# Another order of the calls in front of the loop, on all five engines

## The chip, the cores and the metric

The kernel runs on one core of a Trainium2 chip. The time is the device time of one launch in microseconds (us), the median of several runs. The core has five engines with an instruction queue each: TensorE (PE, matrix products), VectorE (DVE), ScalarE (ACT), GpSimd (POOL) and SyncE (SP), which here only starts transfers. Each queue runs in order; between queues an instruction waits on semaphores.

## The reference

The input t is 16 sequences of 1024 rows of 256 numbers. For each sequence:

```
x = x + layernorm(attention(layernorm(x)))
x = x + layernorm(ffn(layernorm(x)))

attention(t): qkv = t @ W_qkv.T + b_qkv;  Q, K, V = three parts of 256
              softmax(Q @ K.T / 16) @ V
ffn(x):       wg, wu, wd = integer weights / 127     (768 x 256, 768 x 256, 256 x 768)
              (silu(x @ wg.T) * (x @ wu.T)) @ wd.T
```

The norms have no weights and an epsilon of 1e-5.

## The kernel before

The kernel never forms Q and K. It forms A = Wq.T Wk once, z = A x per sequence (`project_z`), and the scores as z times x (`score`). Every factor of a product is split into a high and a low half of 16 bits, and the product is three matmuls: high by high, high by low and low by high. This is why each value is handled several times: ScalarE makes the float value or its high half (`x_hat`, `x_high`, `z_high`, `exp`, `p_high`, `o_high`, `y_hat`, `y_high`, `silu`, `h_high`), and GpSimd or VectorE subtracts to get the low half (`x_low`, `z_low`, `p_low`, `o_low`, `y_low`, `h_low`). SyncE then transposes both halves with a DMA (`turn_x`, `turn_p`, `turn_y`).

The second argument of each call is the sequence b. `x_stats`, `x_norm` and `x_hat` normalise its rows, in two halves g of 512 rows. `score(b, i)` gives the scores of 128 rows against all 1024, i from 0 to 7, in two PSUM banks (the fourth argument is the first bank). `row_max` (VectorE, L708 and L712) finds each row's maximum, `exp` (ScalarE, L491) the exponentials into one of two buffers P, `p_high` (L498) and `p_low` (L374) its halves in one of three buffers. `attend(b, g, u)` is a quarter of P times x for the 512 rows of half g, `project_v` the product with Wv; `y_scale`, `y_stats`, `y_norm`, `x1_add`, `x1_norm` are the first residual sum and its norms. `gate_up(b, g, c)` is one of six chunks of the hidden layer, `h_mul` multiplies gate and up, `down(b, g, pair)` is the last product and `d_stats`, `d_norm`, `d_add`, `add_bias` the second residual sum.

The FFN weights come as integers. Their largest values are found by `ffn_max`, brought into one row by `turn_max` on TensorE, rounded to powers of two by `powers` on VectorE (L616, L619, L621, L624), spread over all partitions by `spread_powers` on TensorE, and turned into scales by `ffn_scales`; `ffn_high` and `ffn_low` make the halves, `turn_ffn` transposes them. `bound` and `V_scales` do the like for the attention's weights.

The order of the work is written out by hand, as a list of calls for each engine: a part in front of the loop, then `for b in range(1, 13)` (ScalarE's from 2 to 13) with one list for all rounds, then a part behind it. A call waits for what it needs by a semaphore count: `exp` of number m waits for `row_max` of m, for `p_low` of m - 2, whose buffer P it takes; `p_high` waits for the transposes of m - 3; `score(b, i, bank, free0, free1)` waits for the two counts that say its banks are free. In the part in front of the loop the engines do sequence 0's attention, then sequence 1's scores woven with sequence 0's attention and its FFN. The lists in the code call helpers, so a line number names a helper's instruction, not its place in the order.

GpSimd takes `x_norm`, all `x_hat_pool`, most `p_low` and `h_low` (VectorE has p_low for i = 1 and 4, `PL_ON_VECTOR`), `z_low` (that of sequence 0 is on VectorE), `x_low`, `y_low` and the norms.

Of the kernel before, what the change touches and what calls it, by code (L numbers as in the profile page):

```python
# [41 lines left out]
def sandwich(nc, x_d, wqkv_d, b_d, wg_d, wu_d, wd_d, out_d):  # L42
# [8 lines left out]
    with ctx:  # L51
# [93 lines left out]
        ffn_scaled, sc2_ready, flag_ready = sem("ffn_scaled"), sem("sc2_ready"), sem("flag_ready")  # L145
# [894 lines left out]
        def _(engine):  # L1040
# [57 lines left out]
            turn_y(s, 0, 0, 1)
            turn_x(s, 2, 1, 0)
            turn_x(s, 2, 1, 1)  # L1100
            load_x(s, 3, 0)
            load_x(s, 3, 1)
            turn_p(s, 1, 5, 0)
            turn_p(s, 1, 5, 1)
            turn_p(s, 1, 6, 0)
            turn_p(s, 1, 6, 1)
            turn_y(s, 0, 1, 0)
            turn_y(s, 0, 1, 1)
            turn_p(s, 1, 7, 0)
            turn_p(s, 1, 7, 1)  # L1110
# [107 lines left out]
        def _(engine):  # L1218
# [5 lines left out]
            x_norm(p, 1, 0)  # L1224
            x_norm(p, 1, 1)
            p_low(p, 0, 0)
            x_hat_pool(p, 1, 1)
            x_low(p, 1, 0)
            p_low(p, 0, 2)
            p_low(p, 0, 3)  # L1230
# [7 lines left out]
            x_norm(p, 2, 1)  # L1238
            z_low(p, 1, 1)
            x_hat_pool(p, 2, 1)  # L1240
            y_norm(p, 0, 0)
            p_low(p, 1, 2)
            p_low(p, 1, 3)
            x1_norm(p, 0, 0)
            x_low(p, 2, 0)
            y_norm(p, 0, 1)
            y_low(p, 0, 0)
            p_low(p, 1, 5)
            x_low(p, 2, 1)
# [9 lines left out]
            z_low(p, 2, 1)  # L1259
            x_norm(p, 3, 0)  # L1260
            h_low(p, 0, 1, 0)
            h_low(p, 0, 1, 1)
            h_low(p, 0, 1, 3)
            x_norm(p, 3, 1)
            h_low(p, 0, 1, 4)
            d_norm(p, 0, 0, 0)
            d_norm(p, 0, 0, 1)
            p_low(p, 2, 0)
# [104 lines left out]
        def _(engine):  # L1373
# [10 lines left out]
            exp(a, 0, 1, 6)  # L1384
            p_high(a, 0, 1)
            x_hat(a, 1, 0)
            x_high(a, 1, 0)
            exp(a, 0, 2, 0)
            p_high(a, 0, 2)
            exp(a, 0, 3, 2)  # L1390
            x_high(a, 1, 1)
            p_high(a, 0, 3)
            exp(a, 0, 4, 4)
            p_high(a, 0, 4)
            exp(a, 0, 5, 6)
            z_high(a, 1, 0, 2)
            p_high(a, 0, 5)
            exp(a, 0, 6, 0)
            p_high(a, 0, 6)
            ffn_high(a, 0)  # L1400
            exp(a, 0, 7, 4)
            p_high(a, 0, 7)
            ffn_high(a, 1)
            exp(a, 1, 0, 0)
            o_high(a, 0, 0, 0)
            p_high(a, 1, 0)
            o_high(a, 0, 0, 1)
# [49 lines left out]
            h_high(a, 0, 1, 3)
            silu(a, 0, 1, 5, 0)
            h_high(a, 0, 1, 4)
            x_hat(a, 3, 0)  # L1460
            h_high(a, 0, 1, 5)
            x_hat(a, 3, 1)
            exp(a, 2, 0, 0)
            p_high(a, 2, 0)
            o_high(a, 1, 0, 1)
            add_bias(a, 0, 0, 0)
            o_high(a, 1, 0, 0)
            add_bias(a, 0, 0, 1)
# [211 lines left out]
        def _(engine):  # L1680
# [9 lines left out]
            x_low(v, 0, 1)  # L1690
            A_low(v)
            c_scales(v)
            V_row_sizes(v)
            bound(v, 1)
            V_scales(v)
            z_float(v, 0, 0, 0)
            z_low(v, 0, 0)
            V_low(v)
            x_stats(v, 1, 0)
            row_max(v, 0, 0, 4)  # L1700
            x_stats(v, 1, 1)
            row_max(v, 0, 1, 6)
# [510 lines left out]
```

## Time and profile before

| | |
|---|---|
| median of 3 runs | 1368.16 us (1368.06 to 1368.95) |
| the profiled execution | 1369.69 us |
| its span, first to last instruction | 1367.9 us |
| mean granted clock of TensorE | 0.997 |
| busy: PE, DVE, ACT, POOL | 1350.2, 901.9, 875.9, 826.5 us |
| DMA, share of 16 engines' span (main queue) | 55.3% |

The profile is of one execution. "Busy" is the time in which an engine works on an instruction; an instruction that waits for a semaphore is not counted, one that has begun and is held up is. A row of the timeline may merge neighbours of one kind (x4) and gives the idle time before it with what ended it. "Releasers" are inferred; where the row says "issue", the profile shows none. PEclk is the granted clock of TensorE as a share of 2.4 GHz.

### The profile page before, as it was taken

What the parts mean: (1) busy time and instruction counts of PE and PEld (TensorE: products, weight loads), DVE (VectorE), ACT (ScalarE), POOL (GpSimd) and SP (SyncE); (2) the same over time, 40 slices, a digit from 0 to 9 for tenths busy, and PEclk for the clock granted to TensorE, in tenths of its full rate; (3) what the DMA queues carried; (4) which work ended last, traced back from release to release, by engine and by line L of the source; (5) the groups of instructions that cost most, each with busy time, mean ns of one, the idle gap of its engine ahead of it and who ended that gap; (6) DMA issues with size and microseconds to landing.
All of it is one profiled execution on the core that took longest, in us unless ns stands there. A gap on an engine that the chain in (4) does not pass through costs nothing.

```text
span 1367.9 us, 22383 instructions
## 1 busy us (share of the span) xinstructions
PE 1350.2 (99%) x7406; PEld 726.3 (53%) x7406; DVE 901.9 (66%) x2169; ACT 875.9 (64%) x1374; POOL 826.5 (60%) x1003
## 2 busy tenths in 40 slices
PE   8999999999999999999999999999999999999998
PEld 4444455554555555555554555545555555555555
DVE  7876565766756667666766666667576676656556
ACT  5667575656756667575675756667566675746645
POOL 4677384674837658476484755748376584754635
PEclk9999999999999999999999999999999999999999
DMA  8995382745728456382764736547373563725512
GB/s 212 198 183 131 72 161 78 128 119 94 146 78 146 94 118 137 78 164 67 133 138 70 162 78 121 126 87 145 85 138 102 112 137 85 136 65 101 108 32 63
DMA packets 437192, 158.29 MB, mean 116 GB/s; under 512 B 418129, under 2 KB 420561, under 8 KB 437074
## 3 DMA queue, kind: packets, MB, share of 16 engines
q1 hardware_dynamic: 436272, 156.03, 55.3%
q8 instruction: 61, 1.00, 0.3%
q10 hardware_dynamic: 802, 0.79, 0.2%
q14 instruction: 57, 0.47, 0.1%
HBM read 36.70 MB, written 16.78 MB: 39 GB/s over the span
## 4 chain that ended last, share of the span: by engine, by line
PE 89%; DVE 4%; SPq 3%; DMA 2%; issue 1%; ACT 1%; POOL 0%; DVEq 0%; ACTq 0%; POOLq 0%
PE S L837 88%; SPq L268 1%; DMA yTl<-yl 1%; DVE mxs L708 1%; SPq L249 1%; DVE S L737 1%; DVE st L746 0%; DVE st L690 0%; SPq L274 0%; DMA xs<-in_L_attn_t 0%; ACT Ph L498 0%; DMA xTl<-xl 0%; SPq L237 0%; DVE zw L701 0%; POOL yl L401 0%
## 5 line engine op out<-in xcount | busy, mean ns | idle before, releaser
L491 ACT ACTIVATE P<-S,nmx,sc 128x1024 f32<-128x1024 f32 x128 | 153.6, 1200 | 285.4 <-DVE nmx L712 285.4
L708 DVE TENSOR_REDUCE mxs<-S 128x1 f32<-128x1024 f32 x128 | 156.0, 1218 | 120.5 <-PE S L837 120.5
L774 DVE SCALAR_TENSOR_TENSOR hf<-S,sc,hf 128x512 f32<-128x512 f32 x192 | 141.8, 745 | 138.7 <-ACT hf L526 133.3
L374 POOL TENSOR_TENSOR Pl<-P,Ph 128x1024 f16<-128x1024 f32 x96 | 204.4, 2130 | 36.0 <-issue 26.3
L837 PE MATMUL S<-xTh,zTh 128*128 128x512 f16 x512 | 194.7, 380 | 4.7 <-ACT P L491 2.2
L837 PE MATMUL S<-xTl,zTh 128*128 128x512 f16 x512 | 194.8, 380 | 0.0
L837 PE MATMUL S<-xTh,zTl 128*128 128x512 f16 x512 | 194.2, 380 | 0.0
L837 PE MATMUL S<-PTh,xh 128*128 128x512 f16 x512 | 194.1, 379 | 0.0
L837 PE MATMUL S<-PTl,xh 128*128 128x512 f16 x512 | 194.0, 379 | 0.0
L837 PE MATMUL S<-PTh,xl 128*128 128x512 f16 x512 | 194.0, 379 | 0.0
L319 POOL TENSOR_SCALAR rs<-mv,sc 128x2 f32<-128x2 f32 (+2 forms) x96 | 35.2, 367 | 231.2 <-DVE mv L750 191.9
L837 PE MATMUL S<-Wh,hTl 128*128 128x256 f16 x768 | 170.3, 273 | 0.0
L837 PE MATMUL S<-Wh,hTh 128*128 128x256 f16 x768 | 170.3, 272 | 0.0
L410 POOL TENSOR_TENSOR hTl<-hf,hTh 128x512 f16<-128x512 f32 x128 | 146.2, 1156 | 39.2 <-ACT hTh L533 39.0
L526 ACT ACTIVATE hf<-S,sc 128x512 f32<-128x512 f32 x192 | 130.6, 681 | 51.9 <-POOL hTl L410 36.1
L323 POOL TENSOR_TENSOR rs<-rs,mhalf 128x4 f32<-128x4 f32 (+2 forms) x160 | 145.3, 908 | 13.4
L837 PE MATMUL S<-yTh,Gh 128*128 128x512 f16 x384 | 145.6, 379 | 3.1 <-DMA yTl<-yl 1.7
L837 PE MATMUL S<-yTl,Gh 128*128 128x512 f16 x384 | 145.5, 379 | 0.0
L837 PE MATMUL S<-yTh,Uh 128*128 128x512 f16 x384 | 145.5, 379 | 0.0
L837 PE MATMUL S<-yTl,Uh 128*128 128x512 f16 x384 | 145.5, 379 | 0.0
L533 ACT ACTIVATE hTh<-hf 128x512 f16<-128x512 f32 x192 | 119.8, 624 | 34.8 <-DVE hf L774 34.8
L498 ACT ACTIVATE Ph<-P 128x1024 f16<-128x1024 f32 x128 | 135.1, 1055 | 3.5
(145 smaller groups left out, 2473.0 us busy)
## 6 DMA issues: line engine op xcount, KB each, us to landing
xs<-in_L_attn_t SPq DMA_DIRECT2D x32, 512.0 KB, 5.5
X<-in_L_attn_t SPq DMA_DIRECT2D x32, 512.0 KB, 4.5
out_x<-X SPq DMA_DIRECT2D x62, 256.0 KB, 2.9
PTh<-Ph SPq DMA_TRANSPOSE x128, 3.3
PTl<-Pl SPq DMA_TRANSPOSE x128, 3.3
hTl<-in_L_ffn_w_gate SPq DMA_DIRECT2D x1, 768.0 KB, 7.8
hTh<-in_L_ffn_w_up SPq DMA_DIRECT2D x1, 768.0 KB, 9.5
hTl<-in_L_ffn_w_down SPq DMA_DIRECT2D x1, 768.0 KB, 10.8
```

Of the source, the lines that this page charges most:

```text
L249: s.engine.dma_start_transpose(dst[k][:, gs, :, :].rearrange("p t d n -> p (t d) n"), src[k][:, gs, :].rearrange("p t d -> p (t d)")).then ...
L319: p.engine.tensor_scalar(rs, var, scalar1=eps, scalar2=mul, op0=ALU.add, **({} if mul is None else {"op1": ALU.mult})).then_inc(g_step, 1)
L323: return p.engine.tensor_tensor(out=rs, in0=rs, in1=mhalf[:, 0:rs.shape[1]], op=ALU.pow)
L374: p.engine.tensor_tensor(out=Pl[:, m % 3, :], in0=P[:, m % 2, :], in1=Ph[:, m % 3, :], op=ALU.subtract).then_inc(pl_vector if i in PL_ON_V ...
L410: p.engine.tensor_tensor(out=hTl[g][:, c, :], in0=hf[:, n % 3, :], in1=hTh[g][:, c, :], op=ALU.subtract).then_inc(hl_vector if c in HL_ON_ ...
L491: a.engine.activation(P[:, m % 2, :], ps[:, bank:bank + 2, :].rearrange("p a n -> p (a n)"), ACT.Exp, bias=nmx[:, c:c + 1], scale=sS, accu ...
L498: a.engine.activation(Ph[:, m % 3, :], P[:, m % 2, :], ACT.Copy).then_inc(ph_done, 1)
L526: a.engine.activation(hf[:, n % 3, :], ps[:, bank, :], ACT.Silu, scale=sc2[:, 3:4]).then_inc(silu_done, 1)
L533: a.engine.activation(hTh[g][:, c, :], hf[:, n % 3, :], ACT.Copy).then_inc(hh_done, 1)
L708: v.engine.tensor_reduce(mxs[:, c:c + 1], ps[:, bank:bank + 2, :].rearrange("p a n -> p (a n)"), axis=AX.X, op=ALU.max, negate=True).then_ ...
L774: v.engine.scalar_tensor_tensor(out=hf[:, n % 3, :], in0=ps[:, bank + 1, :], scalar=sc2[:, 4:5], in1=hf[:, n % 3, :], op0=ALU.mult, op1=AL ...
L837: done = t.engine.matmul(out, s, m, start=(start and i == 0), stop=(stop and i == len(terms) - 1))
```

## The change

Only the order of calls is changed, in the parts in front of the loop of all five lists; calls, helpers, the loop and the part behind it are the same. What a `score` or `gate_up` waits for is changed nowhere. On VectorE, for example, in diff form:

```
+            z_float(v, 0, 0, 0)
+            z_low(v, 0, 0)
             bound(v, 1)
             V_scales(v)
-            z_float(v, 0, 0, 0)
-            z_low(v, 0, 0)
             V_low(v)
+            row_max(v, 0, 0, 4)
             x_stats(v, 1, 0)
-            row_max(v, 0, 0, 4)
-            x_stats(v, 1, 1)
             row_max(v, 0, 1, 6)
             z_float(v, 0, 1, 2)
             row_max(v, 0, 2, 0)
+            x_stats(v, 1, 1)
+            z_low(v, 0, 1)
             p_low(v, 0, 1)
-            z_low(v, 0, 1)
             row_max(v, 0, 3, 2)
...
-            p_low(v, 0, 4)
             z_float(v, 1, 0, 2)
             powers(v, 2, 5, OB[1], 1.0, 1)
+            p_low(v, 0, 4)
+            row_max(v, 0, 7, 4)
             ffn_scales(v)
...
             y_stats(v, 0, 1, 0)
+            row_max(v, 1, 5, 2)
             y_stats(v, 0, 1, 1)
             p_low(v, 1, 4)
-            row_max(v, 1, 5, 2)
-            x1_add(v, 0, 1, 0)
             row_max(v, 1, 6, 0)
             row_max(v, 1, 7, 2)
+            x1_add(v, 0, 1, 0)
             x1_add(v, 0, 1, 1)
             h_mul(v, 0, 0, 0, 6)
-            row_inverse(v, 1, 1)
             z_float(v, 2, 0, 0)
+            x_stats(v, 3, 0)
             h_mul(v, 0, 0, 1, 2)
```

TensorE's list:

```
             score(t, 0, 6, 0, (exp_done, 3), (exp_done, 3))
+            score(t, 0, 7, 4, (exp_done, 5), (exp_done, 5))
             project_z(t, 1, 0, 2, (exp_done, 4), (exp_done, 4))
-            score(t, 0, 7, 4, (exp_done, 5), (exp_done, 5))
             turn_max(t, 2, 5, OB[1], 3, (exp_done, 6))
             attend(t, 0, 0, 0, (exp_done, 6))
             spread_powers(t, 2, 5, OB[1], 1)
             attend(t, 0, 0, 1)
+            attend(t, 0, 0, 2, (ffn_scaled, 6))
             score(t, 1, 0, 0, (exp_done, 7), (exp_done, 7))
-            attend(t, 0, 0, 2, (ffn_scaled, 6))
             attend(t, 0, 0, 3)
+            score(t, 1, 1, 2, None, None)
             project_z(t, 1, 1, 0, (exp_done, 9), (exp_done, 9))
-            score(t, 1, 1, 2, None, None)
...
+            project_z(t, 2, 0, 0, (exp_done, 15), (exp_done, 15))
             gate_up(t, 0, 0, 0, 6, (ol_done[0], 2), (ol_done[1], 2), three)
-            project_z(t, 2, 0, 0, (exp_done, 15), (exp_done, 15))
...
             gate_up(t, 0, 1, 2, 0, (silu_done, 6), (hmul_done, 6), three)
+            down(t, 0, 0, 1, (x1_done, 8), three)
+            down(t, 0, 0, 0, (x1_done, 6), three)
             gate_up(t, 0, 1, 3, 2, (silu_done, 7), (hmul_done, 7), three)
             gate_up(t, 0, 1, 4, 6, (silu_done, 8), (hmul_done, 8), three)
             gate_up(t, 0, 1, 5, 0, (silu_done, 9), (hmul_done, 9), three)
-            down(t, 0, 0, 0, (x1_done, 6), three)
-            down(t, 0, 0, 1, (x1_done, 8), three)
```

On GpSimd `x_hat_pool(1,1)` moves behind `p_low(0,2)`, `x_low(1,0)` and `p_low(0,3)`; `p_low(1,6)`, `p_low(1,7)`, `z_low(2,1)` and `x_norm(3,1)` move to its end, near `p_low(2,0)`. On ScalarE `p_high(0,6)` moves behind both `ffn_high` and `exp(0,7)`, `p_high(1,7)` behind `h_high(0,0,5)`; `exp(0,2)` moves ahead of `p_high(0,1)` and `x_hat(1,0)`. On SyncE `turn_p(1,1,0)` moves ahead of the transposes of the second and third FFN weight, and `turn_p(1,6,1)` and both `turn_p(1,7)` to the end.

VectorE at the start of the program, from `row_max(0,1)` to `z_low(0,1)`: mxs and nmx are a row_max, zw is `z_float`, zTl `z_low`, Pl `p_low`, st and mv `x_stats`. Before:

```order
L708 TENSOR_REDUCE mxs<-S 128x1
L712 TENSOR_SCALAR nmx<-mxs,sc 128x1
L701 TENSOR_SCALAR zw<-S,cb 128x512 x2
L708 TENSOR_REDUCE mxs<-S 128x1
L712 TENSOR_SCALAR nmx<-mxs,sc 128x1
L374 TENSOR_TENSOR Pl<-P,Ph 128x1024
L364 TENSOR_TENSOR zTl<-zw,zTh 128x512 x2
```

and now, the same stretch:

```order
L708 TENSOR_REDUCE mxs<-S 128x1
L712 TENSOR_SCALAR nmx<-mxs,sc 128x1
L701 TENSOR_SCALAR zw<-S,cb 128x512 x2
L708 TENSOR_REDUCE mxs<-S 128x1
L712 TENSOR_SCALAR nmx<-mxs,sc 128x1
L690 BN_STATS st<-xs 128x6 x4
L694 BN_AGGR mv<-st 128x2 x4
L364 TENSOR_TENSOR zTl<-zw,zTh 128x512 x2
L374 TENSOR_TENSOR Pl<-P,Ph 128x1024
```

The second x_stats stood ahead of these rows before and now stands between `row_max(0,2)` and `z_low(0,1)`; p_low has moved behind z_low.

VectorE from `y_scale(0,1)` on (S<-S,rinv,bvb), with `y_stats` (st<-S, mv), `p_low(1,4)` and the row_max of scores (1,5) and after. Before:

```order
L737 SCALAR_TENSOR_TENSOR S<-S,rinv,bvb 128x256 x4
L746 BN_STATS st<-S 128x6 x2
L750 BN_AGGR mv<-st 128x2 x2
L746 BN_STATS st<-S 128x6 x2
L750 BN_AGGR mv<-st 128x2 x2
L374 TENSOR_TENSOR Pl<-P,Ph 128x1024
L708 TENSOR_REDUCE mxs<-S 128x1
L712 TENSOR_SCALAR nmx<-mxs,sc 128x1
L759 SCALAR_TENSOR_TENSOR X<-S,rs,X 128x256 x2
L764 BN_STATS st<-X 128x6 x2
```

and now:

```order
L737 SCALAR_TENSOR_TENSOR S<-S,rinv,bvb 128x256 x4
L746 BN_STATS st<-S 128x6 x2
L750 BN_AGGR mv<-st 128x2 x2
L708 TENSOR_REDUCE mxs<-S 128x1
L712 TENSOR_SCALAR nmx<-mxs,sc 128x1
L746 BN_STATS st<-S 128x6 x2
L750 BN_AGGR mv<-st 128x2 x2
L374 TENSOR_TENSOR Pl<-P,Ph 128x1024
L708 TENSOR_REDUCE mxs<-S 128x1
L712 TENSOR_SCALAR nmx<-mxs,sc 128x1
L708 TENSOR_REDUCE mxs<-S 128x1
L712 TENSOR_SCALAR nmx<-mxs,sc 128x1
```

The first row_max has moved ahead of the second `y_stats` and of p_low, and the first `x1_add` (X<-S,rs,X) behind all three.

ScalarE around `z_high(1,0)` (zTh<-S,cb), with `exp` (P,rsum), `p_high` (Ph) and `x_high(1,1)` (xh<-xs). Before:

```order
L491 ACTIVATE P,rsum<-S,nmx,sc 128x1024
L482 ACTIVATE zTh<-S,cb 128x512 x2
L498 ACTIVATE Ph<-P 128x1024
L491 ACTIVATE P,rsum<-S,nmx,sc 128x1024
L498 ACTIVATE Ph<-P 128x1024
```

and now:

```order
L491 ACTIVATE P,rsum<-S,nmx,sc 128x1024 x2
L475 ACTIVATE xh<-xs 128x1024
L482 ACTIVATE zTh<-S,cb 128x512 x2
L498 ACTIVATE Ph<-P 128x1024 x2
L491 ACTIVATE P,rsum<-S,nmx,sc 128x1024
```

`x_high(1,1)` and `z_high(1,0)` now follow exp(0,5) directly, and p_high(0,4) and p_high(0,5) come behind them.

## Rows read from the trace of the kernel before

**Rows 1.** Page, busy time of the engines and a group of instructions

```profile
PE 1350.2 (99%) x7406; PEld 726.3 (53%) x7406; DVE 901.9 (66%) x2169; ACT 875.9 (64%) x1374; POOL 826.5 (60%) x1003
...
L498 ACT ACTIVATE Ph<-P 128x1024 f16<-128x1024 f32 x128 | 135.1, 1055 | 3.5
```

**Rows 2.** Waits of PE over the whole span: waited for, us in total, times, longest

```profile
PE S L837 <- ACT P L491: 2.2, 1, 2.2
PE S L837 <- DVE zw L701: 2.2, 2, 1.3
...
PE S L837 <- issue: 1.7, 1, 1.7
...
PE S L898 <- DVE pw L624: 0.5, 1, 0.5
```

**Rows 3.** Stretches: length, busy per engine (x), PEclk, DMA share, GB/s

```profile
98.06:101.47 3.41, 3.41 (x9) 1.06 (x7) 0.83 (x2) 2.56 (x4) 3.41 (x3) 0.50 0.63 121
130.00:1355.00 1225.00, 1223.22 (x6771) 661.64 (x6769) 794.84 (x1924) 786.41 (x1241) 737.47 (x899) 1.00 0.53 108
```

**Rows 4.** Timeline of PE: start, us, engine, line, operation, idle before

```profile
28.92 0.39 PE L837 MATMUL S<-xTh,zTh 128*128 128x512 f16 x1 [0.89 <-DVE zw L701]
...
33.34 0.38 PE L837 MATMUL S<-xTh,zTh 128*128 128x512 f16 x1 [1.65 <-issue]
...
50.70 0.39 PE L837 MATMUL S<-PTh,xh 128*128 128x512 f16 x1
...
97.24 0.39 PE L837 MATMUL S<-xTh,zTh 128*128 128x512 f16 x1 [2.18 <-ACT P L491]
...
103.52 0.38 PE L837 MATMUL S<-xTh,Ah 128*128 128x512 f16 x1
...
106.11 0.38 PE L837 MATMUL S<-yTh,Gh 128*128 128x512 f16 x1
...
112.81 0.39 PE L837 MATMUL S<-yTh,Gh 128*128 128x512 f16 x1
```

**Rows 5.** Timeline of VectorE before score(0,4)

```profile
25.17 1.40 DVE L690 BATCH_NORM_STATS2 st<-xs 128x6 f32<-128x256 f32 x4
...
28.12 1.40 DVE L701 TENSOR_SCALAR zw<-S,cb 128x512 f32<-128x512 f32 x2
...
30.82 1.21 DVE L374 TENSOR_TENSOR Pl<-P,Ph 128x1024 f16<-128x1024 f32 x1
31.95 1.28 DVE L364 TENSOR_TENSOR zTl<-zw,zTh 128x512 f16<-128x512 f32 x2
```

**Rows 6.** Timeline of VectorE and ScalarE before score(1,7)

```profile
93.25 1.23 DVE L374 TENSOR_TENSOR Pl<-P,Ph 128x1024 f16<-128x1024 f32 x1
94.39 1.22 DVE L708 TENSOR_REDUCE mxs<-S 128x1 f32<-128x1024 f32 x1
...
95.89 1.20 ACT L491 ACTIVATE P<-S,nmx,sc 128x1024 f32<-128x1024 f32 x1 [0.42 <-DVE nmx L712]
```

**Rows 7.** Timeline of ScalarE, z_high(0,0)

```profile
17.20 1.26 ACT L482 ACTIVATE zTh<-S,cb 128x512 f16<-128x512 f32 x2 [3.40 <-PE S L918]
```

**Rows 8.** Timeline of VectorE and of GpSimd, powers(2,5)

```profile
47.81 1.21 DVE L619 TENSOR_SCALAR ax<-ax 1x3 f32<-1x3 f32 x1
49.06 1.08 DVE L621 TENSOR_SCALAR pw<-ax 1x3 int32<-1x3 int32 x1
...
46.87 2.13 POOL L374 TENSOR_TENSOR Pl<-P,Ph 128x1024 f16<-128x1024 f32 x1 [3.39 <-ACT Ph L498]
48.96 2.27 POOL L364 TENSOR_TENSOR zTl<-zw,zTh 128x512 f16<-128x512 f32 x2
```

**Rows 9.** Line L347, x_hat_pool: ns min/median/max, first and last start

```profile
L347 POOL TENSOR_SCALAR xs<-xs,rs,nb x8: 550/553/2567, 30.9 to 77.3; 128x256 f32<-128x256 f32 x8
```

**Rows 10.** Timeline of ScalarE, first silu; DMA issues at 104 to 106 us

```profile
105.63 1.28 ACT L526 ACT_TABLE_LOAD   x1
...
xs<-in_L_attn_t SPq DMA_DIRECT2D x2, 512.0 KB, 5.0
```

More of the change, by code:

```diff
@@ L1224, in _ @@
             x_norm(p, 1, 0)
+            p_low(p, 0, 0)
             x_norm(p, 1, 1)
-            p_low(p, 0, 0)
+            p_low(p, 0, 2)
+            x_low(p, 1, 0)
+            p_low(p, 0, 3)
             x_hat_pool(p, 1, 1)
-            x_low(p, 1, 0)
-            p_low(p, 0, 2)
-            p_low(p, 0, 3)
             x_low(p, 1, 1)
@@ L1262, in _ @@
             h_low(p, 0, 1, 1)
+            d_norm(p, 0, 0, 1)
             h_low(p, 0, 1, 3)
+            d_norm(p, 0, 0, 0)
+            z_low(p, 2, 1)
+            h_low(p, 0, 1, 4)
+            p_low(p, 1, 6)
+            p_low(p, 1, 7)
+            p_low(p, 2, 0)
             x_norm(p, 3, 1)
[L1265 to L1268, printed above, removed]
             for b in range(1, 13):
@@ L1693, in _ @@
             V_row_sizes(v)
+            z_float(v, 0, 0, 0)
+            z_low(v, 0, 0)
             bound(v, 1)
             V_scales(v)
-            z_float(v, 0, 0, 0)
-            z_low(v, 0, 0)
             V_low(v)
+            row_max(v, 0, 0, 4)
             x_stats(v, 1, 0)
-            row_max(v, 0, 0, 4)
-            x_stats(v, 1, 1)
             row_max(v, 0, 1, 6)
@@ L1746, in _ @@
             y_stats(v, 0, 1, 0)
+            row_max(v, 1, 5, 2)
             y_stats(v, 0, 1, 1)
             p_low(v, 1, 4)
-            row_max(v, 1, 5, 2)
-            x1_add(v, 0, 1, 0)
             row_max(v, 1, 6, 0)
             row_max(v, 1, 7, 2)
+            x1_add(v, 0, 1, 0)
             x1_add(v, 0, 1, 1)
             h_mul(v, 0, 0, 0, 6)
-            row_inverse(v, 1, 1)
             z_float(v, 2, 0, 0)
+            x_stats(v, 3, 0)
             h_mul(v, 0, 0, 1, 2)
@@ L2000, in second_part @@
             gate_up(t, 0, 1, 2, 0, (silu_done, 6), (hmul_done, 6), three)
+            down(t, 0, 0, 1, (x1_done, 8), three)
+            down(t, 0, 0, 0, (x1_done, 6), three)
             gate_up(t, 0, 1, 3, 2, (silu_done, 7), (hmul_done, 7), three)
@@ L2003, in second_part @@
             gate_up(t, 0, 1, 5, 0, (silu_done, 9), (hmul_done, 9), three)
-            down(t, 0, 0, 0, (x1_done, 6), three)
-            down(t, 0, 0, 1, (x1_done, 8), three)
             for b in range(1, 13):
```

180 lines of the change are left out of this document (89 added, 91 removed).

## The prediction

> **What bounds the kernel now.** I read first the busy times of the page: TensorE works 1350.2 of 1367.9 us [rows 1]. So at most 17.7 us can be won, and only where TensorE stands. The waits of PE show where [rows 2]: 2.2 us on an exponential, 2.2 us in two pieces on `z_float`, 1.7 us marked "issue", 0.5 us on the powers. The stretches show that the loop has nothing to give: from 130 to 1355 us PE is busy 1223.22 of 1225.00 us, while one stretch of 3.41 us at 98.06 has a granted clock of 0.50, the lower of the two levels, 1.2 GHz [rows 3]. It comes just after the longest stall of all, 2.18 us, which ends at 97.24 [rows 4]. All the stalls named lie between 28 and 111 us, and the change reorders that part alone. TensorE's instructions are the same in number and kind, so its busy time is no term; the sum is made of stalls.
>
> A project_z, a score or a quarter of attend is twelve matmuls: from 103.52 to 106.11 is 2.59 us; a gate_up of eight takes the 1.73 us that eight starts of 2.59/12 = 0.216 us make [rows 4]. I follow the chain through the new order with these, and write how far TensorE is ahead of the old trace.
>
> **Front, score(0,3) and score(0,4).** VectorE now does `z_float(0,0)` and `z_low(0,0)` ahead of `bound(1)`, and `row_max(0,0)` and `row_max(0,1)` each with one `x_stats` less before them. `x_stats` is (28.12 - 25.17) less one row_max; z_float (1.40, of which 0.08 overlaps) and a row_max fill 28.12 to 30.82, so a row_max is 1.38 and `x_stats` 1.57 [rows 5]; of the row_max 1.22 is the reduction [rows 6]. The old idle time of VectorE before `bound` is replaced by one of like length before `z_float`, since `z_high` starts at 17.20 in both [rows 7] and its first half is needed. By the new list `z_float(0,1)` starts near 27.2 instead of 28.12, and score(0,3), which now starts at 28.92 after 0.89 us of waiting, starts near 28.0. But score(0,4) waits for `z_low(0,1)`: the row "issue" 1.65 at 33.34 comes 0.11 us after zTl's end at 31.95 + 1.28 [rows 4, 5]. In front of it `p_low(0,1)` (1.13 us to the next start) goes and `x_stats(1,1)` (1.57) comes. So: z_low starts at 31.95 - 0.92 + 0.44 = 31.5, ends at 32.75, score(0,4) starts at 32.86. Ahead: 0.48 us. The stall itself grows from 1.65 to about 2.1 us.
>
> **The powers.** project_z(1,0) now follows score(0,7), so five blocks stand between score(0,4)'s start and its end: 32.86 + 5 x 2.59 = 45.8 us. turn_max follows at once, and attend(0,0,0) covers until 49.3. What must be done by then is: half of z_high (1.26/2), half of z_float (1.40/2), and `powers`. In the trace `powers` takes 3.1 us, but two of its operations on three numbers, L619 and L621, take 1.21 and 1.08 us each, and each ends when an operation of GpSimd ends: L619 at 49.02 with the Pl of 46.87 (2.13), L621 at 50.14 with the first half of zTl begun at 48.96 [rows 8]. Undisturbed I price each at 0.2 us, since L712, as small, adds 0.16 us to the reduction of a row_max (1.38 against 1.22). Then `powers` is 0.55 + 3 x 0.2 = 1.15 us. In the new order GpSimd at that time has finished x_low(1,1) (near 47.4), and p_low(0,5) can start only after z_high, p_high(0,4) and p_high(0,5): 46.0 + 0.7 + 2 x 1.06 less 0.1 of overlap, 48.65 [rows 1, 7]. L621 starts near 48.2, 0.4 us before. So I take it that powers is done near 48.6 and TensorE does not stall there at all (before: 0.50). attend(0,0,1) starts at 49.5 instead of 50.70 [rows 4]. Ahead: 1.2 us. The bounds of this term are 0 and -1.8 us: if L621 is caught behind p_low(0,5), the powers come at 51.0 and attend(0,0,1) at 51.3, which is 0.6 us behind the old trace.
>
> The Trainium skill, in "SBUF — State Buffer", section "SBUF: two separate sides", says that VectorE and GpSimd share a pair of ports as an exclusive lock held for a whole instruction, and that the other engine blocks fully. The trace agrees: L619 and L621 took 1.21 and 1.08 us and ended with GpSimd's operations. If instead these durations belonged to the operations themselves, the powers would again take 3.1 us and the saving at the end would be 2.4 us; by the rule it is 4.2 us.
>
> That row of x_hat is the other thing to price: `x_hat_pool(1,1)` takes 4.19 us in the old trace because one of its four operations takes 2567 instead of 550 ns, beside VectorE's Pl and zTl at 30.82 and 31.95 [rows 5, 9]. In the new order it stands after p_low(0,3), near 42 us, beside reductions only: I take 4 x 0.55 = 2.2 us. At 4.19 z_high(1,0) would come 0.7 us later, and the powers with it and caught: the lower bound above.
>
> **From there to score(1,7).** The PE queue is full: every exp, o_low and z_float on the new lists comes before its score, attend or project_v with 0.5 to 3 us to spare, though p_high(0,6) falls behind the two ffn_high, exp(0,7) and so comes 9 us later than before. By SP's queue its transpose and those of p(0,7) have landed near 65.5, and attend(0,1,0) needs them at 67.7. `ffn_low(1)` and (2) also move later, but the FFN transposes are needed only at 97 us. So TensorE reaches score(1,5) 1.2 us ahead. Then comes the large stall. In the old order `row_max(1,5)` starts at 94.39 behind y_stats(0,1,1) and the Pl of 93.25, though its scores are there at 92.5; exp(1,5) follows at 95.89 [rows 6] and score(1,7) at 97.24. Now `row_max(1,5)` stands in front of both: it starts when score(1,5) ends, 0.2 us after 91.1, exp(1,5) at 92.8, done at 94.0, score(1,7) at 94.1, a stall of 0.4 us. Ahead: 3.1 us, and the half clock has no stall of 2.18 us to come after.
>
> **project_z(2,0) and the first gate_ups.** project_z(2,0) now stands before gate_up(0,0,0) and waits for exp(1,6), whose row_max stands behind y_stats and p_low(1,4): 97.4 us against an end of score(1,7) at 96.7: a stall of 0.75. gate_up(0,0,0) at 100.05, gate_up(0,0,1) at 102.1 (exp(1,7), which waits behind z_high), gate_up(0,0,2) after the table load of 1.28 us and one silu [rows 10], near 104.1; gate_up(0,0,3) at 105.8. That would be 5 us ahead (112.81, less its own 1.73, was its time), but gate_up(0,0,4) needs `h_mul(0,0,1)`, and x_stats(3,0) now stands before it. That needs load_x(3), issued after x_low(2,1) at about 101.5, 5.0 us to land [rows 10]: x_stats to 108.7, h_mul to 109.4. The up half of gate_up(0,0,4) starts there instead of at 112.81 + 0.87 = 113.68 [rows 4]. Ahead: 4.2 us. Next in line (silu(0,0,5), h_low(0,0,5) before down(0,0,1) at 119.8) each have 0.2 to 1 us. The two down calls, now before gate_up(0,1,3), fill the time in which silu and p_high(1,7) are made up.
>
> **The sum.** 0.5 + 0.7 + 1.9 + 1.1 = 4.2 us at the start of the loop, less 0.4 us for some eight hand-offs that I priced at nothing (0.05 us each, as the 0.11 us at 33.34 is): 3.8 us. The loop keeps it, since PE there is the bound. Span 1367.9 - 3.8 = 1364.1; the profiled execution took 1369.69 and would take 1365.9. The median shown is 1368.16, 1.53 below that execution: **1364.4 us**. About 0.2% (2.7 us) is what can be told from no change here.
>
> **Rivals.**
> 1. The powers are caught behind GpSimd, by a late x_hat_pool(1,1) or early p_low(0,5). For it: margins of 0.4 us. Against: both L621 and p_low(0,5) follow the same project_z. TensorE is then 0.6 behind at attend(0,0,1), the later stalls fall the same way, and 4.2 - 1.8 = 2.4 remain: 1365.8.
> 2. The stall before score(0,4), 2.1 us, is nearly the 2.18 us after which the clock fell; 1.65 us at the same place left it at 1.00. One stretch of 3.41 us at half clock costs 1.7 us, since work follows without slack: gain 3.8 - 1.7, about 1366.1.
> 3. The gain is given back in the first rounds of the loop: p_low(1,6), p_low(1,7), x_norm(3,1) and reload(1) come 15 to 25 us later than before, so x_hat(3,1) (four operations on ScalarE, some 2.1 us) stands right before exp(2,1). By my chain exp(2,1) ends about 1 us before score(2,3) needs it; if every link is 0.5 us late, TensorE stands about 3 us over the first two rounds: 1367.4. This is also the case that the new order does not do what its replay said.
> 4. Slower: the clock, twice. If the powers are caught, TensorE stands 2.1 us before score(0,4) and 1.8 us before spread_powers. If each is followed by 3.41 us at half clock, 2.4 - 2 x 1.7 = -1.0 us, and every later wait of VectorE's order (project_z(2,0) behind exp(1,6)) is met with nothing in hand, near another 1.5: 1370. It decides where both stalls are followed by the lower clock; with one of them it is rival 1 or 2.
>
> **How the numbers follow.** My forecast 0.46 (its own range 1363.6 to 1365.4); rival 1 0.18; rival 2 0.14; rival 3 0.14; rival 4 0.05; 0.03 that more is won than worked out. Low end 1363.4 takes in the -0.4 that I took off and half a microsecond more; the high end 1367.6 takes in rivals 1 to 3. Faster by over 0.2% is below 1365.4: nearly all of the forecast, the better case, a little of rival 1: 0.53. Within 0.2%: rest of rivals 1, 2 and 3: 0.41. Slower 0.06.
>
> **What would show it.** Right: score(0,4) starts near 32.9; L621 well under 0.5 us and no wait on pw; score(1,7) starts near 94 with a clock of 1.00 throughout; the first matmul of down near 119.8; the loop unchanged, with under 2 us of idle PE. Wrong: a stall over 1 us at spread_powers, a stretch with a clock of 0.50, or waits on exp or yTl inside the loop beyond those of before.

## The result, and the profile after

| | before | after |
|---|---|---|
| median, 12 runs of each on one chip | 1368.11 us (1366.92 to 1368.95) | 1365.51 us (1363.16 to 1366.87) |
| ratio, 95% interval | | 0.998 [0.9972, 0.9988] |
| the profiled execution | 1369.69 us | 1363.82 us |
| its span, mean granted clock | 1367.9 us, 0.997 | 1362.0 us, 0.999 |

The change makes the kernel 2.6 us faster. Two later comparisons of the same kernel on two chips gave 0.9974 [0.9964, 0.9984] and 0.9977 [0.9967, 0.9987], which is 3.7 us each time; the median of all its 30 runs is 1364.42 us. The forecast was 1364.4, a gain of 3.8: the first comparison lies 1.1 us above it, the two later ones at it.

The page, busy times of the engines; TensorE's 1350.2 [rows 1] is 1348.0 now, with the same 7406 matmuls; some 1.7 us of the difference (half of 3.41) is the stretch at half clock below:

```profile
span 1362.0 us, 22384 instructions
...
PE 1348.0 (99%) x7406; PEld 725.5 (53%) x7406; DVE 900.1 (66%) x2169; ACT 875.8 (64%) x1374; POOL 830.3 (61%) x1003
```

The waits of PE after (waited for, total, times, longest), which answer to [rows 2]:

```profile
PE S L837 <- issue: 2.1, 1, 2.1
PE S L837 <- ACT P L491: 1.3, 3, 0.7
PE S L837 <- DVE hf L774: 1.0, 1, 1.0
...
PE S L837 <- DMA yTl<-yl: 0.2, 1, 0.2
```

The two waits on zw are gone; the one marked "issue" is longer than before (1.7); the 2.2 us on an exponential are three short ones; the wait on pw is gone; a wait on hf is new. The stretch that had half clock before and the loop [rows 3]:

```profile
98.06:101.47 3.41, 3.41 (x17) 1.56 (x16) 3.38 (x12) 2.95 (x5) 3.04 (x2) 1.00 1.20 120
...
130.00:1355.00 1225.00, 1224.67 (x6777) 662.18 (x6776) 795.64 (x1920) 789.67 (x1248) 745.12 (x902) 1.00 0.53 110
```

In the 3.41 us from 98.06 on there are seventeen matmuls where there were nine. The timeline of PE at the steps of the prediction (start, us, idle before) answers to [rows 4]:

```profile
32.99 0.38 PE L837 MATMUL S<-xTh,zTh 128*128 128x512 f16 x1 [2.09 <-issue]
...
49.78 0.39 PE L837 MATMUL S<-PTh,xh 128*128 128x512 f16 x1
...
94.36 0.39 PE L837 MATMUL S<-xTh,zTh 128*128 128x512 f16 x1 [0.31 <-ACT P L491]
...
97.86 0.38 PE L837 MATMUL S<-xTh,Ah 128*128 128x512 f16 x1 [0.74 <-ACT P L491]
...
100.45 0.38 PE L837 MATMUL S<-yTh,Gh 128*128 128x512 f16 x1
...
102.58 0.39 PE L837 MATMUL S<-yTh,Gh 128*128 128x512 f16 x1 [0.24 <-ACT P L491]
...
110.10 0.39 PE L837 MATMUL S<-yTh,Uh 128*128 128x512 f16 x1 [1.03 <-DVE hf L774]
...
120.47 0.27 PE L837 MATMUL S<-Wh,hTh 128*128 128x256 f16 x1
...
130.89 0.38 PE L837 MATMUL S<-PTh,xh 128*128 128x512 f16 x1
```

The last row is the loop's first matmul. Before it was this one:

```profile
134.47 0.38 PE L837 MATMUL S<-PTh,xh 128*128 128x512 f16 x1
```

The loop starts 134.47 - 130.89 = 3.58 us earlier. By the waits of PE between 20 and 131 us, its stalls fell by only 2.1 us (6.5 before, 4.4 after); the other 1.5 us are matmuls that ran at half clock before and do not now. VectorE and GpSimd around powers (start, us, operation), the rows that answer to [rows 8]:

```profile
46.03 1.57 DVE L701 TENSOR_SCALAR zw<-S,cb 128x512 f32<-128x512 f32 x2 [1.51 <-ACT zTh L482]
47.53 0.54 DVE L616 TENSOR_REDUCE ax<-S 1x3 f32<-1x384 f32 x1
48.10 0.16 DVE L619 TENSOR_SCALAR ax<-ax 1x3 f32<-1x3 f32 x1
48.29 0.16 DVE L621 TENSOR_SCALAR pw<-ax 1x3 int32<-1x3 int32 x1
48.48 0.16 DVE L624 RECIPROCAL pw<-pw 1x3 f32<-1x3 f32 x1
48.59 1.23 DVE L374 TENSOR_TENSOR Pl<-P,Ph 128x1024 f16<-128x1024 f32 x1
...
41.04 2.19 POOL L347 TENSOR_SCALAR xs<-xs,rs,nb 128x256 f32<-128x256 f32 x4
45.51 2.13 POOL L356 TENSOR_TENSOR xl<-xs,xh 128x1024 f16<-128x1024 f32 x1 [2.28 <-ACT xh L475]
48.84 2.95 POOL L374 TENSOR_TENSOR Pl<-P,Ph 128x1024 f16<-128x1024 f32 x1 [1.21 <-issue]
```

L619 and L621 took 1.21 and 1.08 us and take 0.16 each, in a gap of GpSimd between 47.64 and 48.84. `x_hat_pool(1,1)` takes 2.19 us in all, where one of its four operations alone had taken 2567 ns [rows 9]. The last row shows the other direction: VectorE's Pl begins first, at 48.59, and GpSimd's takes 2.95 instead of 2.13.

VectorE at the new wait, in front of the row of 110.10 (x_stats, then the two h_mul):

```profile
105.30 1.40 DVE L701 TENSOR_SCALAR zw<-S,cb 128x512 f32<-128x512 f32 x2
107.72 1.41 DVE L690 BATCH_NORM_STATS2 st<-xs 128x6 f32<-128x256 f32 x4 [1.02 <-DMA xs<-in_L_attn_t]
109.04 0.36 DVE L694 BATCH_NORM_AGGREGATE mv<-st 128x2 f32<-128x6 f32 x4
109.32 1.38 DVE L774 SCALAR_TENSOR_TENSOR hf<-S,sc,hf 128x512 f32<-128x512 f32 x2
```

### The profile page after: what moved, and what is told of

It is laid out like the page before. It is cut to its first block, busy times and chain, and to the rows that moved or that the text cites. A ratio compares the mean times of both kernels' runs of the same rounds, so it can differ in the third digit from the quotient of the medians.

```text
span 1362.0 us, 22384 instructions
## 1 busy us (share of the span) xinstructions
PE 1348.0 (99%) x7406; PEld 725.5 (53%) x7406; DVE 900.1 (66%) x2169; ACT 875.8 (64%) x1374; POOL 830.3 (61%) x1003
## 4 chain that ended last, share of the span: by engine, by line
PE 91%; SPq 2%; DVE 2%; DMA 1%; POOL 1%; ACT 1%; issue 1%; DVEq 0%; ACTq 0%; POOLq 0%
PE S L837 91%; SPq L268 1%; DMA xs<-in_L_attn_t 1%; SPq L303 1%; DMA yTl<-yl 1%; SPq L249 0%; PE S L918 0%; POOL Pl L374 0%; POOL yl L401 0%; POOL rs L323 0%; DVE st L690 0%; DMA xTl<-xl 0%; ACT Ph L498 0%; DVE S L737 0%; ACT P L491 0%
## 5 line engine op out<-in xcount | busy, mean ns | idle before, releaser
L319 POOL TENSOR_SCALAR rs<-mv,sc 128x2 f32<-128x2 f32 (+2 forms) x96 | 38.1, 396 | 223.0 <-DVE mv L750 186.3
```

What stands on the lines that cost most here:

```text
L319: p.engine.tensor_scalar(rs, var, scalar1=eps, scalar2=mul, op0=ALU.add, **({} if mul is None else {"op1": ALU.mult})).then_inc(g_step, 1)
```

## The experiments

Each kernel is compared with before, and those of two of the three comparisons also with a copy of the changed kernel beside them; h_first, undo, undo_h and held have none. "Low clock" below means an execution whose mean granted clock is 0.998 or less. One more stretch of 3.41 us at half clock lowers the mean by 0.00125. The end of the program is at half clock too, for 0.8 us (busy2) to 3.5 us (before), and the mean is rounded, so this sorting is rough.

### The copy, twice

The changed kernel unaltered, `again` and `again2`.

> The changed kernel once more, with more executions. Theory A (the clock decides between executions): the 2.09 us stall before score(0,4) is followed by a stretch of 3.41 us at a granted clock of 0.50 in some executions and not in others; times fall into two groups 1.7 to 2 us apart, near 1363.5 and 1365.6, the lower group with a mean clock of 0.999 or more. Rival B (DMA jitter in the loop): times spread evenly over 1363 to 1367 and do not follow the clock.

> The changed kernel once more, beside the three others, to see whether its executions fall into two groups by what follows the stall of 2.09 us before score(0,4). Theory A (rival 2 of the prediction, now seen in the traces of three kernels that share this stall: 3.4 us at a granted clock of 0.50 right behind it): where the clock falls, the execution takes 1.5 to 1.8 us more, so two groups near 1363.7 and 1365.5; which of them holds the median changes from one call to the next. Rival (one group, spread by the transfers in the loop): no gap between them.

Measured: 1363.87 (1363.45 to 1365.05, 9 runs) and 1364.43 (1363.88 to 1366.96, 9 runs), beside 1367.52 and 1368.10 of before. With the first comparison there are 30 runs: 21 at a clock of 0.999 or more with a median of 1364.13, and 9 of low clock with a median of 1365.63. The groups are 1.5 us apart, about what one stretch at half clock costs; within the first comparison alone, 7 runs of low clock and 5 of high, 1.9 us. It is not all of the spread: single runs of high clock reach 1366.96. How many runs are of low clock changes from one comparison to the next: 7 of 12, 1 of 9, 1 of 9. So the two groups that were expected inside each of the two copies' comparisons did not show there. Before has both sorts too, 42 of its 80 runs at high clock with 1367.21, 38 of low clock with 1368.28.

The trace of `again2` has the 2.09 us before score(0,4), which starts at 33.42, and a stretch with half clock some 0.7 us later, from 34.14; everything is 0.4 us later there, and the clock was low at the start too, 0.57 on average between 10 and 14 us. The row below begins 0.16 us into the stretch:

```profile
34.30:37.71 3.41, 3.41 (x10) 1.23 (x9) 3.16 (x4) 3.38 (x6) 3.24 (x4) 0.52 0.98 186
```

In the first two traces, of after and `again`, nothing follows the same stall. The remaining spread between executions is in transfers: TensorE's waits for the low half of y (yTl) inside the loop add up to 1.7 us in the trace of before and 0.2 in the trace after, though the loop is the same:

```profile
PE S L837 <- DMA yTl<-yl: 1.7, 4, 0.7
```

### The stall before score(0,4), filled and shortened

`busy` and its repeat `busy2`:

```
             score(t, 0, 3, 2, (zw_done, 3), (zw_done, 4))
+            keep_busy(t, 14, exp_done, 1)
             score(t, 0, 4, 4, (exp_done, 1), (exp_done, 1))
```

`z_first`, on VectorE:

```
             row_max(v, 0, 2, 0)
-            x_stats(v, 1, 1)
             z_low(v, 0, 1)
+            x_stats(v, 1, 1)
```

> Changed kernel with 14 matmuls of 256 columns on constants (some 1.5 us) in the stall before score(0,4), which take no wait away: score(0,4) must still start near 33.0. Theory A: the executions with a stretch at half clock behind this stall vanish, so the median is near that of the faster group of the changed kernel, 1363.6, 1.5 to 2 us below its median of 1365.5. Rival B: no change, 1365.5 with the same spread.

> The changed kernel with 14 matmuls of 256 columns on a constant in front of score(0,4), which fill 1.7 of the 2.09 us in which TensorE stands there; they write a bank that nobody reads then. Theory A (the idle stretch lets the clock fall): no group 1.5 to 1.8 us above, whatever its neighbour shows; median 1363.8 to 1364.6, and never above its neighbour's slower group. Rival (the clock falls for another reason, or the spread comes from elsewhere): the same two groups as its neighbour.

> Changed kernel with x_stats(1,1) moved behind z_low(0,1) on VectorE. By my reading z_low starts 1.6 us earlier, score(0,4) near 31.4 instead of 32.99, the stall there 0.5 us; score(0,7) then waits for exp(0,4) and project_z(1,0) for its transposed x, so 0.8 to 1.0 us are kept at the start of the loop. Theory A: with no stall of 2 us the lower clock before the loop goes away too, so the median falls by 0.8 to 1.0 plus about 1 us, to 1363.4 or less, in one group. Rival B: the median falls by at most 0.9 us and the spread of nearly 4 us stays.

Measured: busy 1364.72 (1363.75 to 1366.96, 11 runs), busy2 1364.33 (1363.56 to 1365.94, 11 runs), z_first 1364.33 (1363.19 to 1366.92, 11 runs), against the copies beside them +0.85, -0.10 and +0.46 us. Both first expectations were missed: 1363.6 for busy, 1363.4 or less for z_first. The filler is in the trace, and score(0,4) keeps its place (busy2):

```profile
30.61 1.69 PE L856 MATMUL S<-ident 128*128 128x256 f16 x14
32.91 0.38 PE L837 MATMUL S<-xTh,zTh 128*128 128x512 f16 x1 [0.61 <-DVE zTl L364]
```

By the times nothing is shown: the copies beside them had one run of low clock each, so there was hardly anything to remove, and the two busy kernels still have 4 such runs among 22. By the traces there is a difference. Eight traces were taken of kernels that keep the stall of 2.09 us (after, again, again2, h_first, undo, undo_h, held, held2), and six of these show half clock right behind it; of the five in which it is filled or shortened (busy, busy2, z_first, both, both2) none does. But the traces come in groups. In the comparison of again, z_first, busy and both none has it, not even again, which keeps the stall; in that of h_first, undo, undo_h and held all keep the stall and all have it. Only the last comparison tells the kinds apart: again2 and held2 have it, busy2 and both2 do not, which comes by chance in one of six draws. So that filling the stall keeps the clock up is suggested and not shown.

The early z_low brings nothing by score(1,7): that starts at 94.25 in z_first and at 94.29 in again. score(0,4) starts 1.6 us earlier, but TensorE then waits for exp(0,4) and for x_low(1,0), whose transfer lands at its old time. The expected 0.8 to 1.0 us were not kept. In both2, which has the same edit:

```profile
31.47 0.38 PE L837 MATMUL S<-xTh,zTh 128*128 128x512 f16 x1 [0.52 <-issue]
...
40.07 0.39 PE L837 MATMUL S<-xTh,zTh 128*128 128x512 f16 x1 [0.67 <-ACT P L491]
43.33 0.39 PE L837 MATMUL S<-xTh,Ah 128*128 128x512 f16 x1 [0.49 <-DMA xTl<-xl]
```

### The wait for load_x(3)

`h_first`, on VectorE:

```
             z_float(v, 2, 0, 0)
-            x_stats(v, 3, 0)
             h_mul(v, 0, 0, 1, 2)
             h_mul(v, 0, 0, 2, 6)
+            x_stats(v, 3, 0)
```

> The changed kernel with x_stats(3,0) put behind h_mul(0,0,2) on VectorE, nothing else. In the changed kernel's trace TensorE stands 1.03 us before the up half of gate_up(0,0,4) at 110.10, because h_mul(0,0,1) is queued behind x_stats(3,0), which itself waits 1.03 us for its load until 107.72. Theory A (the fourth term of the sum is capped by that load): h_mul(0,0,1) comes near 106.6, the stall before 110.10 is gone, the loop starts 1.0 us earlier, and the time is 0.8 to 1.1 us under the changed kernel's copy. Rival (silu, h_high or the next operand is as late, so the stall only changes its releaser): within 0.3 us of it.

Measured: 1362.93 (1362.63 to 1364.62, 5 runs), ratio 0.9965 [0.9952, 0.9979] to a before of 1367.89. The stall on hf is gone from the waits of PE:

```profile
PE S L837 <- issue: 2.1, 1, 2.1
PE S L837 <- ACT P L491: 1.3, 3, 0.7
PE S L918 <- DMA xTl<-xl: 0.6, 1, 0.6
```

It has no copy beside it. Through before, the copy's place there is 0.9974 to 0.9977 of 1367.89, 1364.3 to 1364.7, so the edit is worth about 1.4 to 1.8 us, where 0.8 to 1.1 was expected; the intervals of the ratios overlap, so the excess is not established. The direction has a second witness: both (below) differs from z_first, beside it, by this edit alone and took 1362.99 against 1364.33. So the wait for the load sets the end of the fourth term. Its trace is also one with half clock behind the stall, 0.7 us after score(0,4) starts at 32.93:

```profile
33.60:37.01 3.41, 3.41 (x10) 1.17 (x9) 3.38 (x4) 3.38 (x6) 3.15 (x5) 0.50 0.94 180
```

and that costs 1.7 us on TensorE: score(1,7) starts at 95.99, in again, where the clock held, at 94.29.

### row_max(1,5) put back

`undo` takes back the place of one entry in VectorE's list; `undo_h` does so on h_first.

```
             y_stats(v, 0, 1, 0)
-            row_max(v, 1, 5, 2)
             y_stats(v, 0, 1, 1)
             p_low(v, 1, 4)
+            row_max(v, 1, 5, 2)
```

> The changed kernel with row_max(1,5) put back behind y_stats(0,1,1) and p_low(1,4), where it stood before; nothing else. score(1,7) comes 1.8 to 2.0 us later (96.2 instead of 94.36, stall 2.2). Theory A (the terms of my sum do not add: what score(1,7) wins is swallowed by the wait for the load in front of x_stats(3,0)): the up half of gate_up(0,0,4) still starts near 110.2, and the time is within 0.4 us of the changed kernel's copy, unless the stall is followed by half clock, which adds up to 1.7. Rival (each term counts by itself, +1.9 in the prediction): 1.9 us slower than the changed kernel.

> Both edits of the two kernels beside it: row_max(1,5) back behind p_low(1,4), and x_stats(3,0) behind h_mul(0,0,2). Theory A: without the wait for the load nothing swallows the late score(1,7); it costs 1.3 to 1.6 us against h_first (project_z(2,0) and gate_up(0,0,1) waits give 0.5 of the 1.9 back), so the time lies 0.3 to 0.6 us above the changed kernel's copy. Rival (terms add): 1.9 above h_first. A second rival (everything is capped further down anyway): equal to h_first.

Measured: undo 1366.42 (1365.05 to 1367.73, 11 runs), ratio 0.999 [0.9981, 0.9999]; undo_h 1367.23 (1363.91 to 1368.52, 11 runs), ratio 0.9991 [0.9982, 1.0]. This one place in the list carries more than half of the gain: of the 3.7 us by which the copies lay under before, 1.5 are left. undo_h and h_first, in one comparison, differ by it alone, and their intervals do not meet: [0.9982, 1.0] and [0.9952, 0.9979]. The trace of undo, waits of PE:

```profile
PE S L837 <- ACT P L491: 2.9, 2, 2.6
```

its timeline of PE, score(1,7) and the first matmul of the loop:

```profile
98.28 0.61 PE L837 MATMUL S<-xTh,zTh 128*128 128x512 f16 x1 [2.62 <-ACT P L491]
...
134.37 0.38 PE L837 MATMUL S<-PTh,xh 128*128 128x512 f16 x1
```

and the stretch at that stall:

```profile
98.10:101.51 3.41, 3.23 (x8) 1.19 (x9) 0.17 (x1) 3.31 (x6) 2.23 (x2) 0.50 1.21 189
```

The stall before score(1,7) is back, 2.62 us, and so is the half clock at its end, at the place of [rows 3]; the loop starts at 134.37, where before has 134.47. Of the 3.58 us 3.48 are lost in this execution. score(1,7) is 98.28 - 94.36 = 3.92 us late against the trace after, 2.31 of it the longer stall (2.62 - 0.31) and 1.61 the other half clock, behind score(0,4). From there to the loop: project_z(2,0) no longer waits, -0.74; VectorE reaches x_stats(3,0) after its load has landed, so the wait on hf is gone, -1.03; and the half clock, which by the distance to the loop (36.09 us with 0.24 of waits, against 36.53 with 2.01) costs +1.33. Without the other half clock that is 2.31 - 0.74 - 1.03 + 1.33 = 1.87 us, against medians 1.7 to 2.1 us apart (0.999 less 0.9974 or 0.9977, of 1368). The time alone fits both expectations, theory A with a half clock and the rival's 1.9; the rows decide. The stall is 0.4 longer than the 2.2 expected, since p_low(1,4), now beside `y_low(0,0)` on GpSimd, takes 1.66 us:

```profile
93.86 1.66 DVE L374 TENSOR_TENSOR Pl<-P,Ph 128x1024 f16<-128x1024 f32 x1
...
92.31 2.12 POOL L401 TENSOR_TENSOR yl<-yn,yh 128x1024 f16<-128x1024 f32 x1
```

So the theory that the wait for the load swallows this term was half right: it swallows 1.0 us of it, project_z(2,0) another 0.7, and the clock adds 1.3 on the other side. In undo_h, with nothing left to swallow it, the trace stands where undo's does (first matmul of the loop at 134.39), since undo has no wait left there either. Its median lies 4.3 us above h_first's, where 1.3 to 1.6 was expected, and some 2.7 us above the copy's place, where 0.3 to 0.6 was. By the traces it is 3.07 (134.39 - 131.32), and 1.7 more against an execution of h_first without half clock, as its median run, of clock 0.999, seems to be: 4.8, of which 4.3 are seen. That not every execution of undo_h has both stretches would explain the rest; it is not shown. Why its median is 0.8 above that of undo no trace shows; it stays open.

### GpSimd kept at work during powers

`held` and `held2` add one operation to GpSimd, behind x_low(1,1), whose result nobody reads. held has 1024 columns, held2 1536; lines from 107 on move by one to three (L619 is L622, L621 is L624, L624 is L627).

```
+            p.wait_ge(g_step, 2)
+            p.engine.tensor_tensor(out=fdst[:, :], in0=fsrc[:, :], in1=fsrc[:, :], op=ALU.subtract)
```

> The changed kernel with one more operation on GpSimd, a subtraction of 1024 columns of 16 bits into a tile that nobody reads, some 2 us long, behind x_low(1,1), so that GpSimd is at work while VectorE does powers (47.5 to 48.6 in the changed kernel's trace). Theory A (L619 and L621 are held up by GpSimd's operation, they are not long themselves): one of them ends when a GpSimd operation ends, powers takes 3 to 5 us, TensorE stands 1 to 3 us before spread_powers, and the time is 1 to 3 us above the changed kernel's copy. Rival (the operations on three numbers were long in the old trace for another reason, and are 0.2 us in the new one for that reason): powers still takes 1.1 us, the time is within 0.5 us, since p_low(0,5) 2 us later has slack.

> The changed kernel with a GpSimd operation of 1536 columns of 16 bits, some 2.8 us, behind x_low(1,1), from 47.6 to 50.4 in the changed kernel's time, so that it covers powers (47.5 to 48.6) also where the clock has fallen and everything is 1.6 us late. Theory A (one side is held up while the other works): one of the two operations on three numbers ends when GpSimd's operation ends, the other at the end of the next; powers takes over 3 us, TensorE stands over 1.5 us before spread_powers, the median is 2 to 4 us above the changed kernel's copy. Rival: both stay at 0.2 us, and the time is within 0.5 us of the copy.

Measured: held 1367.69 (1364.97 to 1369.13, 11 runs), ratio 1.0 [0.9991, 1.0009]; held2 1369.38 (1368.22 to 1370.32, 11 runs), ratio 1.0011 [1.0002, 1.002] to before and 4.95 us above its copy, where 2 to 4 was expected. VectorE, GpSimd and then TensorE in held2:

```profile
49.20 0.54 DVE L619 TENSOR_REDUCE ax<-S 1x3 f32<-1x384 f32 x1
49.77 1.05 DVE L622 TENSOR_SCALAR ax<-ax 1x3 f32<-1x3 f32 x1
50.86 2.04 DVE L624 TENSOR_SCALAR pw<-ax 1x3 int32<-1x3 int32 x1
52.94 0.16 DVE L627 RECIPROCAL pw<-pw 1x3 f32<-1x3 f32 x1
...
48.06 2.74 POOL L1236 TENSOR_TENSOR fdst<-fsrc 128x1536 f16<-128x1536 f16 x1
50.77 2.12 POOL L377 TENSOR_TENSOR Pl<-P,Ph 128x1024 f16<-128x1024 f32 x1
...
53.15 0.38 PE L901 MATMUL S<-pw,one 1*128 1x6 f32 x2 [1.94 <-DVE pw L627]
```

L622 ends at 50.82 and GpSimd's filler at 50.80; L624 ends at 52.90 and GpSimd's Pl at 52.89. Both ends agree to 0.02 us, and the length is that of what was left of GpSimd's operation: 1.05 and 2.04 us for three numbers that take 0.16 alone. Not every small operation is held up. The reduction of L619, in the middle of the filler, takes its usual 0.54; it reads a PSUM bank. The reciprocal took 0.16 at 50.17 in the trace of before, while GpSimd's zTl of 48.96 to 51.23 ran [rows 8]. The Trainium skill's page "SBUF — State Buffer", section "SBUF: two separate sides", says that VectorE and GpSimd share a pair of ports, which the first of the two to start holds for its whole instruction, for some forms of VectorE's instructions only. These rows agree, and GpSimd's 2.95 us of the trace after agree nearly: 0.82 more than 2.13, where VectorE's Pl had 49.82 - 48.84 = 0.98 us left.

The stall of 1.94 us is again followed by half clock:

```profile
53.90:57.31 3.41, 3.41 (x10) 1.16 (x9) 3.27 (x13) 1.72 (x3) 2.19 (x2) 0.50 1.09 222
```

This trace has both stretches, the other from 33.45 behind score(0,4). It is rival 4 of the prediction made real by 2.74 extra us on GpSimd, slower than before, 0.6 us under its 1370. Part of the 4.95 us is the clock's: by the traces, 1.7 us for each stretch that an execution of the copy does not have. In held the trace is one in which the clock fell behind score(0,4): powers (49.10 to 50.26) came so late that it met only the last 0.2 us of the shorter filler, and that execution took 1364.97. Nine of the 11 runs took 1367.3 to 1369.1, and these would be the ones that were caught; no trace shows one.

### Both edits

`both` and its repeat `both2`: z_first and h_first together.

> Changed kernel with x_stats(1,1) behind z_low(0,1) and x_stats(3,0) behind h_mul(0,0,2). The second edit takes away the stall of 1.03 us before the up half of gate_up(0,0,4), which ends 0.5 to 1.0 us earlier. If the chain is as I read it, TensorE reaches the loop 1.5 to 2 us earlier than in the changed kernel (130.89 there), and the median is 1362.5 to 1363. If another wait takes the place of h_mul (silu(0,0,3) behind h_low(0,0,0), or h_low(0,0,5) before down), no more than 1 us is won.

> x_stats(1,1) behind z_low(0,1), which leaves 0.52 us of the stall before score(0,4), and x_stats(3,0) behind h_mul(0,0,2), which takes away the stall of 1.03 us. Theory A: one group, 1362.5 to 1363.8, 0.9 to 1.2 us under the faster group of the changed kernel and 2.6 under the slower one. Rival (the better result of the first look was the chip's good hour): the medians of the two differ by under 0.5.

Measured: 1362.99 (1362.54 to 1363.77, 6 runs), ratio 0.9968 [0.9956, 0.998]; and 1363.25 (1362.43 to 1365.18, 7 runs), ratio 0.9967 [0.9956, 0.9978]. The medians are 0.88 and 1.18 us under the copies run beside them, in the ranges expected, and none of the 13 runs is of low clock (of the copies' 18, two). The loop starts at 129.62 and 129.69, 1.3 and 1.2 us before the changed kernel's, where 1.5 to 2 was expected. h_first alone, 1362.93 in one comparison, cannot be told from it: less the 1.7 us of its half clock its loop would start at 129.6 as well, so the gain is that of x_stats(3,0), and z_first adds none that these traces show.

## Why the prediction was right

**score(0,4).** Predicted 32.86 after a stall of 2.1; it starts at 32.99 after 2.09.

**powers.** Predicted done near 48.6 with three operations of 0.2 us, x_hat_pool(1,1) of 2.2 us, and no stall; the rows say 48.64, 3 x 0.16, 2.19, none. That their old length was GpSimd's is shown by held2. The margin that the prediction gave it, 0.4 us between the starts of L621 and p_low(0,5), was 48.84 - 48.29 = 0.55. (Its own terms, 46.0 + 0.7 + 2 x 1.06 - 0.1, give 48.72 for the latter and not 48.65.) attend(0,0,1) starts at 49.78, not 49.5: the ahead was 0.9, not 1.2; 0.13 of the difference stands at score(0,4) already, the rest is as the prediction's hand-offs would be.

**score(1,7).** Predicted 94.1 after a stall of 0.4; it starts at 94.36 after 0.31. The clock held in this trace. undo shows that this place is the largest part of the gain, but not by its 1.9 us alone: two later waits hold 1.8 us of slack against it, and it keeps 1.3 where the clock would fall.

**project_z(2,0), gate_up.** Stall 0.75 predicted, 0.74 in the trace; gate_up(0,0,0) at 100.45 for 100.05, gate_up(0,0,1) at 102.58 for 102.1.

**The clock in the sum.** The prediction says that TensorE's busy time is no term and the sum is made of stalls. That is wrong, and its sum holds the error unseen, since it compares absolute times. It names the half clock that will have no stall to come after, but gives it no term. By the rows the ahead is 0.35 us at score(0,4), 0.92 at attend(0,0,1), 2.88 at score(1,7) and 3.58 at the loop, so the four terms are 0.35, 0.57, 1.96 and 0.70, for 0.5, 0.7, 1.9 and 1.1. In the fourth the stalls grew, from 1.27 to 2.01 us behind score(1,7). What it won, 0.70, is 1.44 us of half clock that before has there [rows 3], less those 0.74. In an execution of before whose clock holds, the change has that much less to win.

**The cap.** The up half of gate_up(0,0,4) was put at 109.4 and starts at 110.10: load_x(3) is issued at 102.88, behind the transposes of x_low(2,1) and of p(1,4) in SyncE's queue, and not near 101.5. The prediction's terms from 101.5 on, 5.0 to land, 1.57 of x_stats and 0.7 of h_mul, give 108.8; the 0.6 more in its 109.4 has no reason there and covered part of the 1.4 by luck. Here TensorE is 3.59 us ahead (its before is 113.69) instead of 4.2, and the first matmul of down starts at 120.47 for 119.8; the 0.4 taken off for hand-offs covers most of that, so the sum, 3.8, came out as 3.58.

**The loop.** It is unchanged, and TensorE's first round runs at the same distance. The spans differ by 5.9 us, not by 3.8: 1.7 - 0.2 of yTl waits and the rest at the end, between two single executions. The forecast of the profiled execution, 1365.9, was therefore 2.1 us too high. The median of the first comparison, 1365.51, was 1.1 above its forecast and just outside that forecast's own range of 1363.6 to 1365.4, close to the 1365.8 and 1366.1 of rivals 1 and 2; it lies well inside the whole range.

**Rival 2** was not refuted but is true part of the time. It asked for 3.41 us at half clock after the stall of 2.1 and priced it at 1.7 us: six of the eight traces with that stall have it (of the changed kernel itself one of three), and its low-clock runs lie 1.5 us above the others. The first comparison, with 7 such runs of 12, came out at 1365.51; the two with one of 9 each at 1363.87 and 1364.43. What the prediction treated as one of two outcomes is a mixture, whose shares change from comparison to comparison, and that 1364.4 is also the median of all 30 runs is luck as much as the sum. What decides on an execution whether the clock falls stays open. Rivals 1 and 3 did not occur in the traces of the changed kernel: no wait on pw, and less waiting in the loop than before.

## What to carry to other kernels

A call's place in a list is worth what TensorE wins there, less the waits behind it that have slack against it: walk the chain to the last cap (here a load that stands late in SyncE's queue) before adding terms. Read a strangely long small operation against the other engine's rows: if it ends with one of GpSimd's to 0.02 us, reordering can take it away, and a margin of 0.55 us is what then holds the gain. Look in the trace of before for stretches at half clock where TensorE works: they are part of what a new order can win, and only in the executions that have them. Near stalls of 2 us a kernel can have two times and not one, so compare medians with the granted clock of each run beside them. And when traces are sorted by kind, see whether the kinds were run side by side.

## What the runs showed of the hardware

A stall of TensorE of 1.94 to 2.62 us between full work was followed by 3.41 us at half clock in ten of twelve cases (six of eight at 2.09, and those of 1.94, 2.18 and twice 2.62), which began between 0.2 us before (undo, 98.09) and 1.2 us after (undo_h, 34.06) the stall's end. Those of 1.65 us [rows 4] and 1.58 us (busy, on hf) and all those of 0.3 to 1.3 us were not. The stretch cost 1.7 us behind score(0,4) (h_first) and 1.3 us behind score(1,7) (undo). Filling 1.69 of the 2.09 us with matmuls of no use left the clock at 1.00 in both traces taken, but so it was in two of the eight traces with the bare stall, one of them run beside busy.

Some operations of VectorE and those of GpSimd hold each other up in both directions. Two operations on three numbers took 1.05 and 2.04 us instead of 0.16 and ended within 0.02 us of GpSimd's instruction; GpSimd's 2.13 became 2.95 us. Three others were not held up: the reduction that reads PSUM (0.54 us in held2), the reciprocal (0.16 us in the trace of before), and the scaling of a row maximum, L712 (0.21 us at 42.93 in the trace after, beside the GpSimd row of 41.04 to 43.23).
